# Window attention: score products of 64 by 64, heads in row halves, key blocks in column halves, and one score slot over two PSUM banks

## The reference

```
q, k, v = split(shift_token(x) @ wqkv)        # 8 heads of 64
q = l2norm(q) * qs;  k = l2norm(k) * ksc
q, k = rotary_xpos(q, k);  q = q * 8
for each window w of 64 queries:              # keys: window w-1 and window w
    sim  = q_w @ [k_(w-1), k_w].T             # 64 x 128
    sim  = where((i < j) | (i > j + 64) | (j == -1), -max, sim)
    out_w = softmax(sim) @ [v_(w-1), v_w]
x = x + out @ wo
```

## Time and profile before

| what | value |
|---|---|
| median of 2 runs | 2051.52 us (2049.68 to 2053.37) |
| the profiled execution | 2051.13 us |
| its span | 2049.3 us |
| mean granted TensorE clock | 0.919 |
| PE busy | 1719.8 us, 84% of the span |
| DVE busy | 1544.9 us, 75% |
| ACT busy | 1363.4 us, 67% |
| POOL busy | 877.9 us, 43% |

### The profile page before, as it was taken

The page is one execution under the profiler, slowest core; times in us unless marked ns, Lnnn a source line. Parts: engine busy times, 40 slices in busy tenths (PEclk is TensorE's granted clock), DMA queues, the critical chain, the costliest instruction groups (busy, mean ns, idle before and its releaser), DMA issues. The chain is left out here.

```text
span 2049.3 us, 39274 instructions
## 1 busy us (share of the span) xinstructions
PE 1719.8 (84%) x12410; PEld 1128.4 (55%) x12410; DVE 1544.9 (75%) x4156; ACT 1363.4 (67%) x4708; POOL 877.9 (43%) x816
## 2 busy tenths in 40 slices
PE   4999999999999955999999695999999683753991
PEld 2555555555555532777777352777777351552660
DVE  2898889988889965899999365899998365663445
ACT  2888888888888862888888222888888226322555
POOL 3555655555655543233233123233233123285555
PEclk9999999999999976999999896999999896755995
DMA  7990000000000000000000100000000100012324
GB/s 205 185 184 11 2 1 2 1 2 1 2 2 2 2 1 6 12 17 12 16 17 12 32 19 6 11 17 13 16 16 13 32 19 1 6 45 66 84 64 133
DMA packets 102525, 65.90 MB, mean 32 GB/s; under 512 B 27698, under 2 KB 93874, under 8 KB 102322
## 3 DMA queue, kind: packets, MB, share of 16 engines
q1 hardware_dynamic: 97970, 54.40, 13.3%
q0 software_dynamic: 4352, 8.99, 1.3%
HBM read 19.50 MB, written 30.24 MB: 24 GB/s over the span
## 5 line engine op out<-in xcount | busy, mean ns | idle before, releaser
L411 ACT ACTIVATE a_E<-a_psS,a_nm 128x128 f32<-128x128 f32 (+1 forms) x1028 | 419.9, 429 | 32.2 <-DVE a_nm L245 30.2
L216 POOL TENSOR_SCALAR a_aT<-a_dT 128x384 f32<-128x384 f32 x256 | 309.1, 1208 | 299.8 <-PE a_psO L529 187.6
L245 DVE TENSOR_REDUCE a_nm<-a_psS 128x2 f32<-128x256 f32 (+1 forms) x514 | 259.9, 546 | 43.9 <-PE a_psS L496 43.4
L492 PE MATMUL a_psS<-a_kT,a_qm 32*128 32x128 f32 (+1 forms) x2064 | 240.6, 351 | 5.4 <-issue 3.4
L270 DVE SCALAR_TENSOR_TENSOR a_d<-a_E,a_cf 128x128 f32<-128x128 f32 (+1 forms) x512 | 219.4, 468 | 27.9 <-DVE a_cf L259 1.4
L411 ACT ACTIVATION_READ_ACCUMULATOR a_E<-a_psS,a_nm 128x1 f32 x1028 | 220.7, 215 | 0.0
L830 POOL TENSOR_TENSOR b0rn<-b0ss,minus_half 128x16 f32<-128x16 f32 x36 | 107.2, 2977 | 223.6 <-DVE b0ss L866 223.6
L830 POOL TENSOR_TENSOR b1rn<-b1ss,minus_half 128x16 f32<-128x16 f32 x36 | 107.2, 2977 | 223.0 <-DVE b1ss L866 223.0
L420 ACT ACTIVATE a_dT<-a_psT 128x384 f32<-128x384 f32 x256 | 127.0, 496 | 73.9 <-PE a_psT L505 71.2
L492 PEld LDWEIGHTS a_psS<-a_kT,a_qm 32*128 32x128 f32 x2064 | 136.6, 186 | 55.9 <-issue 35.6
L505 PE MATMUL a_psT<-ident,a_d 128*128 128x128 f32 x768 | 132.6, 282 | 6.8 <-DVE a_d L270 1.0
(11 more groups left out here) (353 smaller groups left out, 4424.1 us busy)
## 6 DMA issues: line engine op xcount, KB each, us to landing
mx_rows<-mx_blank SPq DMA_DIRECT2D x9, 2080.0 KB, 31.2
mx_xin<-mx_rows SPq DMA_DIRECT2D x72, 65.0 KB
b0v<-b0v SPq DMA_DIRECT2D x34, 128.0 KB, 2.3
b1v<-b1v SPq DMA_DIRECT2D x34, 128.0 KB
F<-mx_results SPq DMA_DIRECT2D x8, 256.0 KB, 5.2
mx_second<-mx_results SPq DMA_DIRECT2D x8, 256.0 KB, 5.4
out_dram<-X SPq DMA_DIRECT2D x8, 256.0 KB, 2.3
f0z<-F SPq DMA_DIRECT2D x9, 128.0 KB
```

The lines of the kernel that those rows point to most:

```text
L216: pool.tensor_scalar(aT[:, s, :], dT[:, s, :], 0.0, None, ALU.max).then_inc(positived.sem, 1)
L245: ins = dve.tensor_reduce(nm[:, s, t, :], psS[:, s, :, (0, P)[t]:(P, 384)[t]], axis=AX.X, op=ALU.max, negate=True)
L411: ins = act.activation(E[:, s, m, c0:c1], psS[:, s, m, c0:c1], ACT.Exp, bias=nm[:, s, t, m:m + 1], accum_out=Z[:, p, h, t, m:m + 1])
L492: pe.matmul(psS[:, s, m, c0:c1], qm[rows, p, a, r, t * P:(t + 1) * P], kT[rows, p, a, 0:c1 - c0], start=(t == 0), stop=False)
```

## The change

Queries are no longer spread with zeros: qT has the same form as kT. A group's scores are eight products of 64 rows (one head's dimensions) by 64 output rows (one window's queries). Head j takes the rows 64j and on, and its scores lie in bank j of psS; the windows 0 and 2 write the partitions 0 to 63, the windows 1 and 3 the partitions 64 to 127, two blocks of 128 columns side by side. Four mask products of 256 columns come first. psS thereby is one slot over two banks, half of each used, and scores(g) waits for the exponentials of g - 1. nm, Z, E, d and dT keep their sizes, with the index n = 2 * head + window // 2. The orders of a step become:

```diff
--- before.py
+++ after.py
@@ -746,7 +746,7 @@
         part = sb("part", [P, 2, 2 * W])
         rot = sb("rot", [P, 2 * W])
         qk = sb("qk", [P, QT, 2 * W])
-        qm = sb("qm", [P, 2, NP, NW, 2, 64])
+        qT = sb("qT", [P, 2, NP, T])
         kT = sb("kT", [P, 2, NP, T])
         v = sb("v", [P, 2, 3, W])
         nm = sb("nm", [P, 2, NW])
@@ -754,7 +754,8 @@
         rz = sb("rz", [P, 2, NW])
         E = sb("E", [P, 2, NW, P])
         d = sb("d", [P, 2, NW, P])
-        dT = sb("dT", [P, 2, NW, 2, 64])
+
+        dT = sb("dT", [P, 2, 2, 2, 2, 64])
         OT = sb("OT", [P, 2, NP, T])
 
         psQ = ps("psQ", [P, 2 * W])
@@ -891,7 +892,8 @@
             def maxima(pair, half, g):
                 s = g % 2
                 dve.wait_ge(scored.sem, scored.at(pair, half, g + 1))
-                dve.tensor_reduce(nm[:, s, :], psS[:, s, :].rearrange("p (w k) -> p w k", k=P), axis=AX.X,
+                dve.tensor_reduce(nm[:, s, :].rearrange("p (j n) -> p j n", n=2),
+                                  psS[:, :, 0:T].rearrange("p j (n k) -> p j n k", k=P), axis=AX.X,
                                   op=ALU.max, negate=True).then_inc(maxed.sem, 1)
 
             def inverse(pair, half, g):
@@ -915,7 +917,6 @@
 
             dve.memset(psO[:, :], 0.0).then_inc(zeroed, 1)
-            dve.memset(qm[:], 0.0).then_inc(zeroed, 1)
             own.begin(dve, 0, 0)
             own.restart(0)
 
@@ -938,8 +939,8 @@
                     own.begin(dve, pair, half)
                     for s in range(NP):
                         k = inverse(pair, half, s)
+                        normalise(pair, half, s, k)
                         maxima(pair, half + (s + 1) // NP, (s + 1) % NP)
-                        normalise(pair, half, s, k)
                         if s == 0:
                             scale(pair, half - 1, 1, misc_full.at(pair, half, 0))
                             norms(pair, half, 0)
@@ -961,15 +962,15 @@
                 act.wait_ge(maxed.sem, maxed.at(pair, half, g + 1))
                 act.wait_ge(mixed.sem, mixed.at(pair, half, g - 1))
                 for n in range(NW):
-                    ins = act.activation(E[:, s, n, :], psS[:, s, n * P:(n + 1) * P], ACT.Exp, bias=nm[:, s, n:n + 1],
-                                         accum_out=Z[:, s, n:n + 1])
+                    ins = act.activation(E[:, s, n, :], psS[:, n // 2, n % 2 * P:(n % 2 + 1) * P], ACT.Exp,
+                                         bias=nm[:, s, n:n + 1], accum_out=Z[:, s, n:n + 1])
                 ins.then_inc(exped.sem, 1)
 
             def evac_d(pair, half, g):
                 s = g % 2
                 act.wait_ge(turned.sem, turned.at(pair, half, g + 1))
                 act.wait_ge(pved.sem, pved.at(pair, half, g - 1))
-                act.activation(dT[:, s].rearrange("p w j q -> p (w j q)"), psT[:, :], ACT.Copy)\
+                act.activation(dT[:, s].rearrange("p j n c q -> p (j n c q)"), psT[:, :], ACT.Copy)\
                    .then_inc(evaced.sem, 1)
 
             def move_ot(pair, half, g, p):
@@ -991,15 +992,10 @@
                     ins = act.activation(hT[64:P, p, 1:T], psM[64:P, m, 0:T - 1], ACT.Copy)
                 elif use in (U_V0, U_V2):
                     ins = act.activation(v[:, p, 2 * (use == U_V2), :], psM[:, m, :], ACT.Copy)
-                elif use in (U_TQ0, U_TQ1):
-                    n = 2 * (use == U_TQ1)
-                    for j in range(2):
-                        rows = slice(64 * j, 64 * j + 64)
-                        ins = act.activation(qm[rows, p, :, n:n + 2, j, :],
-                                             psM[rows, m, :].rearrange("p (g w q) -> p g w q", w=2, q=64), ACT.Copy)
                 else:
-                    c = P * (use == U_TK1)
-                    ins = act.activation(kT[:, p, :, c:c + P], psM[:, m, :].rearrange("p (n t) -> p n t", t=P), ACT.Copy)
+                    c = P * (use in (U_TQ1, U_TK1))
+                    to = qT if use in (U_TQ0, U_TQ1) else kT
+                    ins = act.activation(to[:, p, :, c:c + P], psM[:, m, :].rearrange("p (n t) -> p n t", t=P), ACT.Copy)
                 ins.then_inc(misc_free.sem, 1)
 
             act.wait_ge(zeroed, 1)
@@ -1007,7 +1003,7 @@
                 act.sem_inc(signal.sem, n)
             for n, (use, batch) in enumerate(PEELED):
                 if use == U_TQ0:
-                    act.wait_ge(zeroed, 3)
+                    act.wait_ge(zeroed, 2)
                     act.wait_ge(cleared, 3)
                 use_copy(use, batch % 2, misc_full.early(n + 1), n % 2)
                 if n < 2:
@@ -1020,12 +1016,12 @@
                 for half in range(2):
                     copy = lambda use: use_copy(use, 1 - half, misc_full.at(pair, half, use + 1), bank(use))
                     for s in range(NP):
-                        exps(pair, half + (s + 1) // NP, (s + 1) % NP)
                         if s in (0, 2):
                             square(pair, half, s // 2)
                         if s != 2:
                             copy((U_TQ0, U_TQ1, None, U_V2)[s])
                         evac_d(pair, half, s)
+                        exps(pair, half + (s + 1) // NP, (s + 1) % NP)
                         if s < 2:
                             copy((U_TK0, U_TK1)[s])
                         if s == 3:
@@ -1039,12 +1035,18 @@
         @block.tensor
         def _(pe):
             def scores(pair, half, g):
-                s, p = g % 2, half % 2
-                pe.wait_ge(exped.sem, exped.at(pair, half, g - 1))
-                pe.matmul(psS[:, s, :], identb[:, :], behind[:, :], start=True, stop=False)
-                for n in range(NW):
-                    ins = pe.matmul(psS[:, s, n * P:(n + 1) * P], qm[:, p, g, n].rearrange("p j q -> p (j q)"),
-                                    kT[:, p, g, KEYS[n]:KEYS[n] + P], start=False, stop=(n == NW - 1))
+                p = half % 2
+                pe.wait_ge(exped.sem, exped.at(pair, half, g))
+                for j in range(2):
+                    for c in (slice(0, 64), slice(64, P)):
+                        pe.matmul(psS[c, j, 0:T], identb[:, c], behind[:, :], start=True, stop=False)
+
+                for n in range(2):
+                    for w in range(2 * n, 2 * n + 2):
+                        for j in range(2):
+                            head, half_of = slice(64 * j, 64 * j + 64), slice(64 * (w % 2), 64 * (w % 2) + 64)
+                            ins = pe.matmul(psS[half_of, j, n * P:(n + 1) * P], qT[head, p, g, 64 * w:64 * w + 64],
+                                            kT[head, p, g, KEYS[w]:KEYS[w] + P], start=False, stop=(n == 1))
                 ins.then_inc(scored.sem, 1)
 
             def turn(pair, half, g):
@@ -1062,11 +1064,11 @@
                 out = lambda j: psO[64 * j:64 * j + 64, :]
                 vh = lambda j, t: v[:, p, t, (2 * g + j) * HD:(2 * g + j + 1) * HD]
                 for j in range(2):
-                    pe.matmul(out(j)[:, 0:P], vh(j, 0), dT[:, s, 0:2, j, :], start=True, stop=True)
+                    pe.matmul(out(j)[:, 0:P], vh(j, 0), dT[:, s, j, 0, :, :], start=True, stop=True)
                 for j in range(2):
-                    pe.matmul(out(j)[:, P:192], vh(j, 1), dT[:, s, 2, j, :], start=True, stop=True)
+                    pe.matmul(out(j)[:, P:192], vh(j, 1), dT[:, s, j, 1, 0, :], start=True, stop=True)
                 for j in range(2):
-                    ins = pe.matmul(out(j)[:, 192:T], vh(j, 2), dT[:, s, 3, j, :], start=True, stop=True)
+                    ins = pe.matmul(out(j)[:, 192:T], vh(j, 2), dT[:, s, j, 1, 1, :], start=True, stop=True)
                 ins.then_inc(pved.sem, 1)
 
             def project(pair, half, t):
@@ -1117,10 +1119,9 @@
                     pe.wait_ge(misc_free.sem, misc_free.early(4))
                     project(0, -1, 0)
             pe.wait_ge(misc_free.sem, misc_free.early(PRE))
-            pe.wait_ge(zeroed, 3)
+            pe.wait_ge(zeroed, 2)
             pe.wait_ge(cleared, 3)
             scores(0, 0, 0)
-            scores(0, 0, 1)
             project(0, -1, 1)
             project(0, 0, 0)
             for pair in range(LAST):
@@ -1130,10 +1131,9 @@
                     use = lambda u: use_misc(u, misc_free.at(pair, half, u - 1 + (u in (U_V2, U_HT))), 1 - half,
                                              bank(u))
                     for s in range(NP):
-                        if s == 2:
-
+                        if s == NP - 1:
                             pe.wait_ge(misc_free.sem, misc_free.at(pair, half, U_TK1 + 1))
-                        scores(pair, half + (s + 2) // NP, (s + 2) % NP)
+                        scores(pair, half + (s + 1) // NP, (s + 1) % NP)
                         if s < 2:
                             pe.wait_ge(qk_ready.sem, qk_ready.at(pair, half - 1, s + 1))
                         if s != 2:
@@ -2062,10 +2062,16 @@
 
         casts = []
```

(10 more changed lines are left out.)

## The result

The changed kernel takes 2269.19 us (2269.07 to 2269.3, 2 runs) against 2051.52: 1.106 times the time before, interval 1.103 to 1.109, 217.7 us more. The forecast was 2239 us, slower, with 2190 to 2320 as its range.

The account below looks back on a forecast made before the run. No single engine had much room before; afterwards a closed chain of PE, DVE and ACT hand-overs would bound each batch. 2051 + 193 (32 batches at +6.0) - 5 (layer openings) = 2239 us, range 2190 to 2320.

Parts of the forecast that it names:

- The circle: In each batch, six forced links between PE, DVE and ACT queues close into a loop: 25.21 us against 19.19.
- the walk: Adding up old-timeline spacings link by link through a batch's in-order queues, giving 25.21 us a batch.
- 1.27 us a group: PE's score group after the change: 1.04 us for sixteen passes plus 0.23 for masks, against 1.10 before.
- A: DVE from arrival of scores(1) through maxima, scale, norms, normalise and maxima(2) to the end of rotate: 8.12 us.
- C: DVE from maxima(3) through scale, norms, normalise and the next batch's maxima to the end of the residual: 6.14 us.
- D: PE after the residual: hand-over, V2, turn(3) and hand-over, 1.65 us.
- Granted clock at 1.00: Expected sign in the changed kernel's loop: PE's clock stays at full 2.4 GHz.
- R1: Rival, chance 0.22: PE's clock falls around V2 and the next projection; mean 0.85 adds 1.3 us a batch, 2282 us.
- the openings: Start of each layer, one score group and two half copies less before the loop: -5 us in all.
- R2: Rival, chance 0.08: products on array quarters don't overlap, 1.94 us more work in the circle; 2301 us.
- R3: Rival, chance 0.03: waits are absorbed and DVE's work bounds at 17.6 us a batch; 1995 us.
- R4: Rival, chance 0.09: hT copy or residual not awaited, some 2 us a batch less; 2175 us.

Follow-up runs that it names:

- experiments 4: Changed kernel with ACT copying hT before the exponentials of the next batch's group 0; 2217.17 us, ratio 1.082.
- experiment 5: Changed kernel with DVE adding the residual before the maxima of the next batch's group 0; 2223.24 us, ratio 1.086.
- experiment 6: Changed kernel with both the hT copy ahead of the exponentials and the residual ahead of the maxima at s = 3; 2195.53 us, ratio 1.073.
- 9: Kernel of experiment 8 with six spare bf16 products ahead of each score group; 2274.47 us, ratio 1.111.
- 10: Kernel of experiment 8 with eight spare products behind V0 of step 0; 2226.99 us, ratio 1.087.
- experiment 11: Changed kernel with residual first, hT copy first, and 12 and 4 spare products in PE's two pauses of step 3; 2171.9 us, ratio 1.061.
- Experiment 2: Kernel before, with its two slots and products, only the new orders on DVE and ACT; 2199.03 us, ratio 1.074.
- Experiment 3: Changed kernel, one slot kept, with the old orders on DVE and ACT; 2252.43 us, ratio 1.100.
- experiment 1: Kernel before, with its old products and two query copies, but one score slot and the new orders; 2284.99 us, ratio 1.116.
- experiment 8: Changed kernel with spare products in PE's pauses of step 3, 16 before V2's wait and 8 before the hT wait; 2229.24 us, ratio 1.089.

## Why the prediction was right, and where it was off

*The circle.* Right, and shown: experiments 4, 5, 6, 9 and 10 each take away or add work at a named place, and the batch follows the walk within 0.15 us, counted at equal clock (the walk before experiment 11 was 0.3 us short). Five of the six links were within 0.3 us in the table above.

*The products.* The term "1.27 us a group" was too large: measured 0.94 (0.34 for the masks, 0.60 for sixteen passes), 0.037 us a pass. The step that failed is "I take 16 x 0.065": two halves of the array overlap in pairs, as in the earlier trace rows, but quarters overlap further. The masks went the other way, 0.34 where 0.23 was taken. The Trainium skill (TensorEngine Tiling (Array Packing), Theoretical Speedup) has up to two times for one dimension of at most 64, which makes up to four for both. That was nearer: against 0.11 us for a pass of 128 by 128 the sixteen passes run at three times. Twice 0.33 us less in the circle is 0.66 a batch, -21 us.

*The other links* came out a little longer: a projection ahead of the narrower mask products holds PE 1.91 us, not 1.82 (twice a batch), and A, C and D were each 0.07 to 0.11 longer. Together the circle is 24.86 us against 25.21: -11 us for all 32 batches.

*The clock.* "Granted clock at 1.00" was wrong. I had left it to the rival R1 with 0.22, because no pause is as long as those before the falls in the earlier trace rows. It fell in seven of twelve batches, and the falls cost 34 to 40 us. That is R1's mechanism at about the size I gave it for a mean clock of 0.85 (+1.3 a batch; measured +1.06 at 0.92), because the slow stretch covers the projection and the mask products that stand in the circle. The case to forecast was the circle and the clock together, not the one or the other.

*The sum.* 2239 - 11 + 34 = 2262. Of the other 7 us some 4 lie behind the second layer, in parts that the change leaves as they were: from the end of its last output projection to the end of the span it is 460.6 us against 456.1. Why is not known. The rest lies in the layers, where I had taken off 5 for the openings and at most part of it was gained.

That the forecast came within some 30 us is in part luck: the products were taken 21 us too dear, which hid part of what the clock cost. With the right price for them it would have been 2218.

*One slot and the orders.* The forecast laid the circle to the slot ("before, links A to C and C to D were cut by the second slot"). Experiment 2 shows this to be half of it: with two slots the new orders alone close a circle of 23.33 us. Experiment 3 shows the other half: one slot with the old orders takes 25.58. Either alone loses; together they take hardly more time than the worse of them (2269 against 2252 us), and the circle itself is shorter (24.86 against 25.58).

*R2, R3 and R4* are out: the quarters overlap; DVE, busy 192.7 of 280 us, is far from the bound; and both the residual and the hT copy are awaited in every batch, as the table of waits shows. (In R2, 1.94 us is the price of a batch, not of each group.) The saved query copy is worth nothing visible, as said: ACT stands idle over 40% of the loop, and experiment 1, which has the old copy, shows no cost for it.

## What to carry to other kernels

A second buffer between engines with in-order queues can be worth more than the work that its memory saves, as here: count the longest closed path of hand-overs through a batch, following every engine's queue, before giving one up. Such a walk needs only the spacings of the old timeline, and it told the new batch time at full clock within 1.5%. Where the change opens pauses on TensorE in front of work that stands on that path, add a price for the clock, and test for it by filling the pauses with spare products.

## What the runs showed of the hardware

At full clock the pauses of step 3 are the same in every batch of the changed kernel: 2.56 us, then 2.9 us of which PE works 2.6, then 1.41 us. The clock fell in seven of twelve batches (twice as in the batch at 921.44, five times already between the pauses) and not in the other five (as at 1077.59). The length of the pauses alone doesn't tell when it falls. With 1.75 and 0.26 us (experiment 3) it didn't in the twelve batches counted, but did later, at the end of the first of these pauses; with 1.10 and 1.41 us (experiment 2) it fell in four of thirteen; with 1.96 and 1.41 us (experiment 5) in four of fourteen; with 1.96 and 0.26 us (experiment 6) in eleven of thirteen. The first row is of experiment 3 (1.13 us at full clock), the second of experiment 2 (1.98 at full clock):

```profile
1176.21 2.08 PE L1096 MATMUL b0psM<-wv,b0hT 128*128 128x512 f32 x2 [1.75 <-DVE F L915]
...
864.53 3.65 PE L1077 MATMUL b0psQ<-wqk,b0hT 128*128 128x512 f32 x4 [1.41 <-ACT b0hT L991]
```

With 0.71 and 0.43 us left by the filler it didn't fall in the first layer's loop (experiment 8); these two rows are the filler kernel's:

```profile
916.44 1.13 PE L1100 MATMUL b0psM<-wv,b0hT 128*128 128x512 f32 x2 [0.71 <-DVE F L915]
...
920.76 1.99 PE L1083 MATMUL b0psQ<-wqk,b0hT 128*128 128x512 f32 x4 [0.43 <-ACT b0hT L992]
```

Sixteen fp32 passes of 64 by 64 with 128 columns hold PE 0.60 us (903.59 - 902.99), where eight of 128 by 128 took 0.89 for the same scores.
